# Normalising a column copy of x on GpSimd, with mean and rstd spread by DMA, in place of ScalarE's row form and TensorE's transposes

## The chip, the cores and the metric

One core of one Trainium2 chip. The metric is the device time of the whole kernel in microseconds, median over runs. Engines are named TensorE (PE in the rows, PEld its weight loads), VectorE (DVE), ScalarE (ACT), GpSimd (POOL) and SyncE (SP, which here only issues DMAs).

## The reference, cut to what matters

A block with cross attention and a top-2 mixture of experts. The change touches only how `_layernorm(x)` reaches the q projection of the attention.

```python
def _layernorm(x, axis=-1, eps=1e-05):
    m = jnp.mean(x, axis=axis, keepdims=True)
    v = jnp.var(x, axis=axis, keepdims=True)
    return (x - m) / jnp.sqrt(v + eps)

def _L0_xattn_ref(q, k, v, w_qs, w_ks, w_vs, w_proj, b_proj):
    qh = jnp.einsum('bld,hdk->hblk', q, w_qs)      # 16 heads, D = 256, d_k = 64
    kh = jnp.einsum('bld,hdk->hblk', k, w_ks)      # k, v: 64 rows of context per batch
    vh = jnp.einsum('bld,hdk->hblk', v, w_vs)
    attn = jax.nn.softmax(jnp.einsum('hblk,hbmk->hblm', qh, kh), axis=-1)
    out = jnp.einsum('hblm,hbmk->hblk', attn, vh) * qh
    out = out.transpose(1, 2, 0, 3).reshape(q.shape[0], q.shape[1], -1)
    return out @ w_proj.T + b_proj

x = x + jnp.tanh(g_xattn[0]) * _L0_xattn_ref(_layernorm(x), ctx_1024, ctx_1024, ...)
x = x + jnp.tanh(g_ffn[0]) * _L0_ffn_ref(_layernorm(x), ...)   # 8 experts, 2 per token
```

x is (4, 1024, 256) in float32.

## The kernel before, in words

The program has two stages. The first is the attention; the second runs 71 blocks of 128 routed rows through the experts. All of the change lies in the first.

**Tiling.** The 4096 tokens are cut into 8 groups `g` of 512 (`NG`), and each group into `TG` = 4 tiles of 128. The 16 heads make 8 pairs `p` (`NP`). One step of the attention handles pair `p` of group `g`, and every engine's program has a `step` function that is written out for all 64 steps. `n` is the running number of the pair. The steps are a hand-made software pipeline: in the step of pair n TensorE projects q for n, makes scores for n-1, transposes probabilities for n-4, multiplies by v for n-5 and projects out for n-6. Small jobs are hung on fixed steps of a group: layernorm of the next group, the second layernorm and routing of the group two back, and a piece of an expert's weights, split into two float16 halves, in each step.

**How the normalised x reaches q.** Rows of x are loaded to `xin`. VectorE takes statistics in `ln1` (four `bn_stats`, in step p = 1 for the next group) and `ln1_moments` (p = 2); GpSimd raises the variance to -1/2 in `ln_rstd` (p = 3); VectorE makes `shift` in `ln1_shift_of` (p = 4); ScalarE writes `xn` in `ln1_apply` (p = 4 and 5); TensorE transposes `xn` into the PSUM bank `job_ps` in `x_transpose` (ends of p = 5 and 6); ScalarE and VectorE take the high and low float16 halves `xt_h`, `xt_l` in `split_x` (p = 6 and 7), and `project_q` of the next group waits for the last `xt_lo`. In group 0 `job_ps` is also the bank of `project_k`, so that `project_k(6)` and `(7)` wait for `split_x` to have read it.

**VectorE's step**, in order: `residual` (p = 6), `exp_sum` for pair n-3 (`esum`, `rinv`), the small jobs, `score_max` and `score_sub` for pair n-1 (`smax`, `ssub`), `times_q` for n-5 (`r`), `expert_lo` (`split`). The small jobs of steps 3 and 4 are the two halves of `choose` (the routing, chains of ops on 128x32), that of step 5 is `place`. TensorE's `scores` for pair n-1 wait for `score_sub` of pair n-2, since `s_ps` is one buffer.

**GpSimd's step**: `normalize` for n-3 (`pn`), then `ln_rstd`, one `scatter` of records by an indirect DMA (from group 2 on), `product_lo` for n-5 (`r_l`), which waits for ScalarE's `r_h`. TensorE uses `pn` and `r_l` one step later.

**SyncE** issues in the order written in `group`; a wait in it holds all that follows.

Of the kernel before, what the change touches and what calls it, by code (L numbers as in the profile page):

```python
# [22 lines left out]
F32 = mybir.dt.float32  # L23
# [48 lines left out]
def build(nc, x, ctxt, g_xattn, g_ffn, wq, wk, wv, wproj, bproj, gate, w1, w2, out):  # L72
    dram = dict(
        x=x, ctxt=ctxt, g_xattn=g_xattn, g_ffn=g_ffn, wq=wq, wk=wk, wv=wv, wproj=wproj, bproj=bproj, gate=gate, w1=w1, w2=w2,
# [4 lines left out]
        w_split=nc.dram_tensor("w_split", (E, P, 2, WN), F16, kind="Internal").ap(),  # L79
    )  # L80
# [168 lines left out]
def attention(nc, ctx, dram, carry, weights):  # L249
# [41 lines left out]
    xn = sb("xn", [P, TG, D], F32)  # L291
# [26 lines left out]
    wp_sb = q32[:, 4:8, :].rearrange("p a g -> p (a g)").rearrange("p (c n) -> p c n", c=KD)  # L318

# [31 lines left out]
    ln1_ops, ln1_rstd, ln1_shift, xn_done, xt_tp, xt_hi, xt_lo = (sem(n) for n in ("ln1_ops", "ln1_rstd", "ln1_shift", "xn_done", "xt_tp", "xt_hi", "xt_lo"))  # L351
# [74 lines left out]
    def _(sp):  # L426
# [82 lines left out]
        for c in range(B // 2):  # L509
            double_v(c)  # L510
# [15 lines left out]
    def _(pe):  # L526
# [37 lines left out]
        def project_k(p):  # L564
# [114 lines left out]
        def small_job(g, k, p):  # L679

            if p == 1 and known(g, 2):
                x2_transpose(g - 2, k, 0)
# [67 lines left out]
    def _(act):  # L750
# [3 lines left out]
        def ln1_apply(g, par, tiles=range(TG)):  # L754
            if tiles[0] == 0:
                act.wait_ge(ln1_shift, g)
                after(act, xt_tp, 2 * g)
            for t in tiles:
                last = nc.scalar.activation(xn[:, t, :], xin[:, par, t, :], ACT.Identity, bias=shift[:, 0, t:t + 1], scale=rstd[:, 0, t:t + 1])
            if tiles[-1] == TG - 1:  # L760
                last.then_inc(xn_done, 1)

        def split_x(g, par, k, bank):

            act.wait_ge(xt_tp, 2 * g + k + 1)
# [17 lines left out]
        for k in range(KD):  # L783
            split_x(0, 0, k, (q_ps, pt_ps)[k])
# [86 lines left out]
        def step(b, g, k, p, pairs_back=LAST):  # L871
# [4 lines left out]
            if p in (6, 7) and has_next(g):  # L876
                split_x(g + 1, 1 - k, p - 6, job_ps)
# [54 lines left out]
    def _(dve):  # L932
# [22 lines left out]
        def ln1_shift_of(g):  # L955
            dve.wait_ge(ln1_rstd, g + 1)
            nc.vector.scalar_tensor_tensor(shift[:, 0, :], mv[:, 0, :, 0], -1.0, rstd[:, 0, :], ALU.mult, ALU.mult).then_inc(ln1_shift, 1)

        def split_x(g, par, k, bank):
# [20 lines left out]
        for k in range(KD):  # L980
            split_x(0, 0, k, (q_ps, pt_ps)[k])
# [111 lines left out]
        def step(b, g, k, p, pairs_back=LAST):  # L1093
# [82 lines left out]
    def _(pool):  # L1176
# [45 lines left out]

        def scatter(g, par, i):
# [10 lines left out]
        def step(g, k, p, pairs_back=LAST):  # L1234
# [474 lines left out]
```

## Time and profile before

| | |
|---|---|
| median of 3 runs | 795.76 us (794.93 to 798.36) |
| the profiled execution | 796.72 us, of which its span, first to last instruction, is 794.6 us |
| attention stage | about the first 370 us of the span |
| TensorE, VectorE, GpSimd, ScalarE busy over the span | 93%, 77%, 53%, 48% |
| mean granted TensorE clock | 0.987 of full speed |

Shares are averages over both stages. What a step costs is to be read inside the attention stage, in the stretches of single groups (a group lasts some 42 us), by who waits for whom.

### The profile page before, as it was taken

How to read it: one execution, taken by the hardware profiler on the slowest of the kernel's cores; microseconds unless marked ns; L12 is line 12 of the kernel's file. 1: busy time of each engine (PE TensorE's matmuls, PEld its weight loads, DVE VectorE, ACT ScalarE, POOL GpSimd, SP SyncE). 2: the span in 40 equal slices, each digit the busy share in tenths (PEclk: the TensorE clock that was granted, in tenths of full speed). 3: DMA queues.
4: the chain of work that ended last, by engine and by line, in shares of the span. 5: the costliest groups of instructions: out<-in, count | busy, mean ns of one | idle time of the engine just before them, and what ended most of it. 6: DMA issues, size and time to landing. Idle time of an engine off the chain costs nothing. (4 is left out here: it accounts for less than half of the span.)

```text
span 794.6 us, 23823 instructions
## 1 busy us (share of the span) xinstructions
PE 740.1 (93%) x8020; PEld 615.9 (78%) x8021; DVE 610.5 (77%) x1305; ACT 382.5 (48%) x680; POOL 417.3 (53%) x380
## 2 busy tenths in 40 slices
PE   4979999999999999987799998999999999999991
PEld 2657777676767777755798887899999999999991
DVE  6668889999898989794777778877777777777760
ACT  3566776767666676653344432333333333333330
POOL 3124454757676666645434475645555555555542
PEclk9999999999999999999899999999999999999997
DMA  8543242627272534423688866433333333333321
GB/s 268 160 108 132 80 161 92 234 81 265 74 255 93 208 113 175 139 100 87 207 217 229 233 161 125 76 54 47 48 52 50 49 46 53 50 50 47 51 32 20
DMA packets 94104, 93.74 MB, mean 118 GB/s; under 512 B 59216, under 2 KB 77840, under 8 KB 94032
## 3 DMA queue, kind: packets, MB, share of 16 engines
q1 hardware_dynamic: 32400, 65.89, 25.0%
q0 software_dynamic: 13392, 18.03, 13.0%
q10 hardware_dynamic: 48240, 8.87, 7.0%
q8 instruction: 43, 0.70, 0.4%
q14 instruction: 29, 0.24, 0.1%
HBM read 53.76 MB, written 37.95 MB: 115 GB/s over the span
## 5 line engine op out<-in xcount | busy, mean ns | idle before, releaser
L1399 PE MATMUL h_ps<-bx_h,w_now 128*128 128x128 f16 x2272 | 195.4, 220 | 12.5 <-DVE bx_l L1536 12.4
L1412 PE MATMUL pair_ps<-weights,ht_h 128*128 x1136 | 190.7, 273 | 2.5 <-DVE ht_l L1550 1.8
L1399 PEld LDWEIGHTS h_ps<-bx_h,w_now 128*128 128x128 f16 x2272 | 153.0, 98 | 17.3 <-DVE bx_l L1536 15.2
L1399 PE MATMUL h_ps<-bx_l,w_now 128*128 128x128 f16 x1136 | 157.0, 220 | 0.0
L1412 PE MATMUL pair_ps<-weights,ht_l 128*128 x568 | 154.9, 273 | 0.0
L1656 POOL DMA_INDIRECT out<-y,meta x71 | 144.3, 2032 | 15.7 <-issue 8.8
L1221 POOL TENSOR_TENSOR r_l<-r,r_h 128x512 f16<-128x512 f32 x64 | 74.3, 1161 | 104.8 <-ACT r_h L835 104.8
L1655 POOL TENSOR_TENSOR wait_mark<-wait_mark 128x1 f32<-128x1 f32 x71 | 40.3, 567 | 163.3 <-DMA out<-y,meta 101.9
L1412 PEld LDWEIGHTS pair_ps<-weights,ht_h 128*128 128x128 f16 x1136 | 110.0, 97 | 18.2 <-issue 3.6
L1475 ACT ACTIVATE y<-pair_ps,meta 128x256 f32<-128x256 f32 x71 | 33.6, 473 | 175.6 <-DVE bx L1525 75.8
L1548 DVE CAST ht_h<-hid 128x1024 f16<-128x1024 f32 x71 | 49.4, 696 | 73.2 <-ACT hid L1468 73.2
L1468 ACT ACTIVATE hid<-h_ps 128x1024 f32<-128x1024 f32 x71 | 72.5, 1022 | 51.1 <-PE h_ps L1399 51.1
L1550 DVE TENSOR_TENSOR ht_l<-hid,ht_h 128x1024 f16<-128x1024 f32 x71 | 87.0, 1226 | 2.4
L1399 PEld LDWEIGHTS h_ps<-bx_l,w_now 128*128 128x128 f16 x1136 | 87.6, 98 | 0.0
L1542 DVE COPY w_now<-weights 128x4096 f16 x71 | 86.8, 1222 | 0.0
L1215 POOL TENSOR_TENSOR pn<-ex,rinv 128x512 f32<-128x512 f32 x64 | 66.4, 1038 | 38.6 <-DVE rinv L1021 38.6
L609 PEld LDWEIGHTS s_ps<-kb,q 128*128 128x128 f32 x512 | 67.3, 193 | 13.8 <-issue 5.8
L609 PE MATMUL s_ps<-kb,q 128*128 128x128 f32 x512 | 68.6, 278 | 2.8 <-DVE ssub L1012 2.8
L651 PE MATMUL pair_ps<-wp_h,r_h 128*128 128x256 f16 x256 | 61.3, 275 | 2.5 <-DVE x_even L1034 2.4
L835 ACT CAST r_h<-r 128x512 f16<-128x512 f32 x64 | 39.4, 616 | 45.0 <-DVE r L1027 44.1
L651 PE MATMUL pair_ps<-wp_l,r_h 128*128 128x256 f16 x256 | 60.7, 273 | 0.0
L1412 PEld LDWEIGHTS pair_ps<-weights,ht_l 128*128 128x128 f16 x568 | 55.5, 98 | 5.2
(260 smaller groups left out, 1326.8 us busy)
## 6 DMA issues: line engine op xcount, KB each, us to landing
stage<-in_w SPq DMA_DIRECT2D x16, 1024.0 KB, 8.7
w_split<-split SPq DMA_DIRECT2D x14, 1024.0 KB, 6.1
weights<-w_split SPq DMA_DIRECT2D x14, 1024.0 KB, 5.9
rows<-records ACTq DMA_DIRECT2D x268, 32.0 KB
xin<-in_x SPq DMA_DIRECT2D x8, 512.0 KB, 4.9
x_even<-in_x SPq DMA_DIRECT2D x4, 512.0 KB, 3.6
x_odd<-in_x SPq DMA_DIRECT2D x4, 512.0 KB, 3.6
out<-x_even SPq DMA_DIRECT2D x4, 512.0 KB, 2.7
```

Of the source, the lines that this page charges most:

```text
L609: last = nc.tensor.matmul(s_ps[:, t].rearrange("p h m -> p (h m)"), q32[:, p, t * P:(t + 1) * P], kb[:, b, p, :] if isinstance(b, int) els ...
L651: nc.tensor.matmul(pj_ps[:, t, :], r_h[:, p % 2, t * P:(t + 1) * P], wt[:, p, :], start=(p == 0 and i == 0 and t % 2 == 0), stop=False, sk ...
L1215: nc.gpsimd.tensor_tensor(pn[:, p % 2].rearrange("p h t m -> p t h m"), ex[:, p % 2].rearrange("p t (h m) -> p t h m", h=2), rinv[:, p % 2 ...
L1221: nc.gpsimd.tensor_tensor(r_l[:, p % 2, :], r32[:, p % 2, :], r_h[:, p % 2, :], ALU.subtract).then_inc(r_lo, 1)
L1399: last = nc.tensor.matmul(h_ps[r % 2][:, c, :], w1_now[:, r % 2, s, k * F + c * P:k * F + c * P + P], xt[:, r % 2, k, :], start=(j == 0 an ...
L1412: last = nc.tensor.matmul(y_ps[r % 2], ht[:, r % 2, c, :], weights_at(e, s, WN // 2 + c * D, D).rearrange("p o n -> p (o n)"), start=(c == ...
L1468: nc.scalar.activation(hid[:, r % 2], h_ps[r % 2][:, :, :], ACT.Silu, scale=1.0 / WS).then_inc(h_act, 1)
L1542: nc.vector.tensor_copy(w1_now[:, r % 2], weights[:, bass.ds(e, 1), :, 0:KD * F].rearrange("p o s n -> p (o s) n")).then_inc(w1_ready, 1)
L1548: nc.vector.tensor_copy(ht_h[:, r % 2], hid[:, r % 2]).then_inc(h_hi, 1)
L1550: nc.vector.tensor_tensor(ht_l[:, r % 2], hid[:, r % 2], ht_h[:, r % 2], ALU.subtract).then_inc(h_lo, 1)
L1655: nc.gpsimd.tensor_tensor(wait_mark[:, 1:2], wait_mark[:, 0:1], wait_mark[:, 0:1], ALU.add).then_inc(mark_set, 1)
L1656: pool.indirect_dma_start(out, bass.IndirectOffsetOnAxis(meta[:, r, 0:1].bitcast(U32), 0), y[:, r % 2, :], None, compute_op=ALU.add).then_ ...
```

## The change

The host also gives x by columns: `xt[g, d, k, t, q]` in DRAM, so that one group is a tile `xt_in` of 128 partitions x (2 x 512). For groups 1 to 7:

- SyncE loads `xt_in` (`load_xt`, 512 KB), writes mean and rstd of the group (8 numbers per partition) to DRAM and, when that has landed, reads them back spread over all partitions as `mean_rstd` (128 x 1024 numbers, 512 KB; `spread_moments`).
- GpSimd subtracts the mean and multiplies by rstd in place: `centre_x` and `scale_x`, each a `tensor_tensor` on 128x512 once per half `k`, so four per group, in steps 3, 4, 5 and 6 (in group 0: two each in steps 5 and 6). The operand from `mean_rstd` is read with a step of 8 numbers.
- `split_x` on ScalarE and VectorE reads `xt_in` in SBUF in place of `job_ps` in PSUM.
- ScalarE's `ln1_apply`, VectorE's `ln1_shift_of` and TensorE's 14 calls of `x_transpose` go, with the waits around `job_ps`; group 0 still goes through `xn`.
- `ln1` moves from step 1 to step 0, `ln1_moments` from 2 to 1, `ln_rstd` from 3 to 1 (in group 0 they stay). SyncE's order within a group changes.

```diff
+        def load_xt(g):
+            if g == 1:
+                sp.wait_ge(xt_tp, KD)
+            else:
+                sp.wait_ge(xt_lo, KD * g)
+            sp.dma_start(xt_in[:, :, :], dram["xt"][g]).then_inc(xt_loaded, 16)
+
+        def spread_moments(g):
+            sp.wait_ge(ln1_rstd, g + 1)
+            row = dram["moments"][g % 2]
+            sp.dma_start(row.rearrange("(p n) -> p n", p=P), mv[:, 0, :, :].rearrange("p t s -> p (t s)")).then_inc(moments_out, 16)
+            sp.wait_ge(moments_out, 16 * g)
+            after(sp, x_normed, 2 * KD * (g - 1))
+            sp.dma_start(mean_rstd[:, :, :, :].rearrange("p q t s -> p (q t s)"), row.partition_broadcast(P)).then_inc(moments_in, 16)
...
         def group(g, par):
-            load_residual(g, par)
+            if known(g, 1) and has_next(g):
+                load_xt(g + 1)
             if not isinstance(g, int) or g + 2 < NG:
                 load_x(g + 2, par)
+            if known(g, 1) and has_next(g):
+                spread_moments(g + 1)
+            load_residual(g, par)
+            if known(g, HELD):
+                store_split(g, 0)
+            if has_next(g):
+                load_w1(g + 1)
             if known(g, 1):
                 store_x1(g - 1, 1 - par)
...
# TensorE
             after(pe, k_placed, 2 * p)
-            if p == 6:
-                pe.wait_ge(xt_lo, KD + 1)
-            if p == 7:
-                pe.wait_ge(xt_lo, 2 * KD)
...
-            if p == 5 and has_next(g):
-                x_transpose(g + 1, 0, job_ps)
-            if p == 6 and has_next(g):
-                x_transpose(g + 1, 1, job_ps)
...
# ScalarE
-            if p == 4 and has_next(g):
-                ln1_apply(g + 1, 1 - k, range(TG if first else TG // 2))
-            if p == 5 and has_next(g) and not first:
-                ln1_apply(g + 1, 1 - k, range(TG // 2, TG))
             if p in (6, 7) and has_next(g):
-                split_x(g + 1, 1 - k, p - 6, job_ps)
+                split_x(g + 1, 1 - k, p - 6, xt_in[:, p - 6, :])
...
# VectorE
-            if p == 4 and has_next(g):
-                ln1_shift_of(g + 1)
-            if p == 1 and has_next(g):
+            if p == (1 if first else 0) and has_next(g):
                 ln1_of(b, g, k)
-            if p == 2 and has_next(g):
+            if p == (2 if first else 1) and has_next(g):
                 ln1_moments(g + 1)
...
# GpSimd
+        def centre_x(g, k):
+            if k == 0:
+                pool.wait_ge(xt_loaded, 16 * g)
+                pool.wait_ge(moments_in, 16 * g)
+            x = xt_in[:, k, :].rearrange("p (t q) -> p t q", t=TG)
+            nc.gpsimd.tensor_tensor(x, x, mean_rstd[:, :, :, 0].rearrange("p q t -> p t q"), ALU.subtract).then_inc(x_normed, 1)
...
-            if p == 3 and has_next(g):
+            if p == (3 if g == 0 else 1) and has_next(g):
                 ln_rstd(0, g + 1, ln1_ops, ln1_rstd)
+            if p == (5 if g == 0 else 3) and has_next(g):
+                centre_x(g + 1, 0)
+            if p == (5 if g == 0 else 4) and has_next(g):
+                scale_x(g + 1, 0)
+            if p == (6 if g == 0 else 5) and has_next(g):
+                centre_x(g + 1, 1)
+            if p == 6 and has_next(g):
+                scale_x(g + 1, 1)
```

**GpSimd, steps 3, 4 and 5 of group 3, before.** `pn` opens each step and `r_l` ends it; the DMAs are the scatters.

```order
L1215 TENSOR_TENSOR pn<-ex,rinv 128x4x2x64
L1194 TENSOR_TENSOR rstd<-vare,minus_half 128x4
L1231 DMA records<-rec_odd,slot_odd 33920x258
L1221 TENSOR_TENSOR r_l<-r,r_h 128x512
L1215 TENSOR_TENSOR pn<-ex,rinv 128x4x2x64
L1231 DMA records<-rec_odd,slot_odd 33920x258
L1221 TENSOR_TENSOR r_l<-r,r_h 128x512
L1215 TENSOR_TENSOR pn<-ex,rinv 128x4x2x64
L1229 TENSOR_TENSOR wait_mark<-wait_mark 128x1
```

The same steps after the change:

```order
L1219 TENSOR_TENSOR pn<-ex,rinv 128x4x2x64
L1233 TENSOR_TENSOR xt_in<-xt_in,mean_rstd 128x512
L1249 DMA records<-rec_odd,slot_odd 33920x258
L1225 TENSOR_TENSOR r_l<-r,r_h 128x512
L1219 TENSOR_TENSOR pn<-ex,rinv 128x4x2x64
L1239 TENSOR_TENSOR xt_in<-xt_in,mean_rstd 128x512
L1249 DMA records<-rec_odd,slot_odd 33920x258
L1225 TENSOR_TENSOR r_l<-r,r_h 128x512
L1219 TENSOR_TENSOR pn<-ex,rinv 128x4x2x64
L1233 TENSOR_TENSOR xt_in<-xt_in,mean_rstd 128x512
L1247 TENSOR_TENSOR wait_mark<-wait_mark 128x1
```

One 128x512 operation (L1233 centres, L1239 scales) now stands right behind each `pn`; the small `rstd` op has gone to step 1.

**VectorE, step 4 of group 3, before**: the end of `exp_sum`, the shift, and the second half of `choose`.

```order
L1018 TENSOR_REDUCE esum<-ex 128x8
L1021 RECIPROCAL rinv<-esum 128x8
L957 SCALAR_TENSOR_TENSOR shift<-mv,rstd 128x4
L207 TENSOR_REDUCE top<-lg 128x4
L208 TENSOR_TENSOR cand<-lg,top 128x32
L209 SCALAR_TENSOR_TENSOR cand<-cand,iota_e 128x32
L210 TENSOR_REDUCE choice<-cand 128x4
L211 TENSOR_TENSOR mask<-iota_e,choice 128x32
```

The same place after:

```order
L1023 TENSOR_REDUCE esum<-ex 128x8
L1026 RECIPROCAL rinv<-esum 128x8
L209 TENSOR_REDUCE top<-lg 128x4
L210 TENSOR_TENSOR cand<-lg,top 128x32
L211 SCALAR_TENSOR_TENSOR cand<-cand,iota_e 128x32
L212 TENSOR_REDUCE choice<-cand 128x4
L213 TENSOR_TENSOR mask<-iota_e,choice 128x32
```

Only `shift` has gone; the chain of small routing ops is as it was.

**SyncE, from the second weight load of one group to the first store of the next, before:**

```order
L448 DMA stage<-in_w 128x8x256
L456 DMA x_odd<-in_x 128x1024
L460 DMA xin<-in_x 128x1024
L464 DMA out<-x_even 128x1024
L471 DMA w_split<-split 256x1x2048
```

and after:

```order
L455 DMA stage<-in_w 128x8x256
L471 DMA xt_in<-in_xt 128x1024
L486 DMA xin<-in_x 128x1024
L477 DMA moments<-mv 128x8
L480 DMA mean_rstd<-moments 128x1024
L463 DMA x_even<-in_x 128x1024
L497 DMA w_split<-split 256x1x2048
```

Two loads of x now follow the weight load at once, then the two transfers of the moments, and only then the residual and the next group's stores.

## Rows read from the trace of the kernel before

**Rows 1.** 125 to 165 us: busy PE, PEld, DVE, ACT, POOL, clock, DMA.

```profile
125.00:165.00 40.00, 39.64 (x342) 29.18 (x341) 36.69 (x99) 27.97 (x53) 25.53 (x26) 1.00 0.49 168
```

**Rows 2.** What TensorE waited for, 85 to 345 us: total, times, longest.

```profile
PE s_ps L609 <- DVE ssub L1012: 1.0, 5, 0.2
```

**Rows 3.** Timeline of TensorE, group 3: start, length, idle before.

```profile
175.66 0.71 PE L533 MATMUL job_ps<-ident,xn 128*128 128x128 f32 x4
176.21 0.59 PE L599 MATMUL q_ps<-xt_h,wq_h 128*128 128x512 f16 x2
...
180.84 0.65 PE L533 MATMUL job_ps<-ident,xn 128*128 128x128 f32 x4
181.32 0.60 PE L599 MATMUL q_ps<-xt_h,wq_h 128*128 128x512 f16 x2
...
187.61 1.13 PE L609 MATMUL s_ps<-kb,q 128*128 128x128 f32 x8 [0.20 <-DVE ssub L1012]
```

**Rows 4.** Timeline of VectorE, groups 2 (end) and 3.

```profile
151.02 1.35 DVE L942 BATCH_NORM_STATS2 stats<-xin 128x6 f32<-128x256 f32 x4
...
163.44 0.69 DVE L1007 TENSOR_REDUCE smax<-s_ps 128x8 f32<-128x512 f32 x1 [0.59 <-PE s_ps L609]
...
166.91 0.44 DVE L957 SCALAR_TENSOR_TENSOR shift<-mv,rstd 128x4 f32<-128x4 f32 x1
...
167.49 0.90 DVE L208 TENSOR_TENSOR cand<-lg,top 128x32 f32<-128x32 f32 x1
...
168.86 0.19 DVE L211 TENSOR_TENSOR mask<-iota_e,choice 128x32 f32<-128x32 f32 x1
...
173.23 1.09 DVE L232 TENSOR_TENSOR mask<-pos,mask 128x32 f32<-128x32 f32 x2
...
174.34 0.13 DVE L235 TENSOR_TENSOR seen<-seen,mtiles 128x8 f32<-128x8 f32 x1
...
183.57 0.64 DVE L962 TENSOR_TENSOR xt_l<-job_ps,xt_h 128x512 f16<-128x512 f32 x1
...
186.78 0.69 DVE L1012 TENSOR_TENSOR ssub<-s_ps,smax 128x512 f32<-128x512 f32 x1
```

**Rows 5.** Timeline of GpSimd, group 3.

```profile
160.86 1.04 POOL L1215 TENSOR_TENSOR pn<-ex,rinv 128x512 f32<-128x512 f32 x1
...
166.19 1.15 POOL L1221 TENSOR_TENSOR r_l<-r,r_h 128x512 f16<-128x512 f32 x1 [2.04 <-ACT r_h L835]
167.30 1.04 POOL L1215 TENSOR_TENSOR pn<-ex,rinv 128x512 f32<-128x512 f32 x1
...
173.14 1.03 POOL L1215 TENSOR_TENSOR pn<-ex,rinv 128x512 f32<-128x512 f32 x1
...
182.97 1.15 POOL L1221 TENSOR_TENSOR r_l<-r,r_h 128x512 f16<-128x512 f32 x1 [0.95 <-ACT r_h L835]
```

**Rows 6.** L208 in both stages: shortest, median, longest in ns, first and last start.

```profile
L208 DVE TENSOR_TENSOR cand<-lg,top x12: 191/340/902, 119.3 to 336.5; 128x32 f32<-128x32 f32 x12
L208 DVE TENSOR_TENSOR last_cand<-last_lg,last_top x4: 191/192/193, 416.4 to 460.0; 128x32 f32<-128x32 f32 x4
```

**Rows 7.** DMA issues, 140 to 170 us: size, us to landing.

```profile
stage<-in_w SPq DMA_DIRECT2D x1, 1024.0 KB, 8.7
x_odd<-in_x SPq DMA_DIRECT2D x1, 512.0 KB, 3.5
xin<-in_x SPq DMA_DIRECT2D x1, 512.0 KB, 4.5
```

**Rows 8.** SyncE's timeline: the weight load that ends group 2's issues.

```profile
147.02 0.61 SPq L448 DMA_DIRECT2D stage<-in_w  x1
```

**Rows 9.** Timeline of TensorE in group 0.

```profile
50.15 2.04 PE L574 MATMUL job_ps<-x2t,rec_even 128*128 128x256 f32 x4 [2.90 <-DVE xt_l L962]
...
59.12 1.10 PE L574 MATMUL job_ps<-x2t,rec_even 128*128 128x256 f32 x4 [1.35 <-DVE xt_l L962]
```

**Rows 10.** Timeline of VectorE at the start of group 1.

```profile
65.63 0.69 DVE L1018 TENSOR_REDUCE esum<-ex 128x8 f32<-128x512 f32 x1
```

More of the change, by code:

```diff
@@ L79, in build @@
         w_split=nc.dram_tensor("w_split", (E, P, 2, WN), F16, kind="Internal").ap(),
+        moments=nc.dram_tensor("moments", (2, G * 2), F32, kind="Internal").ap(),
     )
@@ L290, in attention @@
     shift = sb("shift", [P, 2, TG], F32)
-    xn = sb("xn", [P, TG, D], F32)
+    xt_in = sb("xt_in", [P, KD, G], F32)
+    mean_rstd = sb("mean_rstd", [P, P, TG, 2], F32)
     xt_h, xt_l = (sb(f"xt_{s}", [P, 2, KD, G], F16) for s in "hl")
@@ L318, in attention @@
     wp_sb = q32[:, 4:8, :].rearrange("p a g -> p (a g)").rearrange("p (c n) -> p c n", c=KD)
+    xn = xt_in[:, :, :].rearrange("p k g -> p (k g)").rearrange("p (t d) -> p t d", t=TG)
     ctx_t = x2t[:, :, 0:B // 2 * 3 * M].rearrange("p k (c j m) -> p k c j m", c=B // 2, j=3)
@@ L508, in _ @@
         load_w2(0)
-        for c in range(B // 2):
-            double_v(c)
+        load_xt(1)
+        double_v(0)
+        spread_moments(1)
+        double_v(1)
         for k in range(GB):
@@ L681, in small_job @@
             if p == 1 and known(g, 2):
+                if g > 2:
+                    pe.wait_ge(routed.pos_read, g - 2)
                 x2_transpose(g - 2, k, 0)
@@ L752, in _, with split_x @@
         nc.scalar.activation(esum[:, 0, 0, 0:1], ident[:, 0:1], ACT.Exp)
[L754 to L765, printed above, removed]
+        def split_x(g, par, k, x):
+            if g == 0:
+                act.wait_ge(xt_tp, k + 1)
+            else:
+                act.wait_ge(x_normed, 2 * (KD * (g - 1) + k + 1))
             if known(g, 2):
                 act.wait_ge(q_mm, pair_no(g - 2, NP))
-            nc.scalar.copy(xt_h[:, par, k, :], bank[:, :]).then_inc(xt_hi, 1)
+            nc.scalar.copy(xt_h[:, par, k, :], x).then_inc(xt_hi, 1)
         def split_wq(half):
@@ L783, in _ @@
         for k in range(KD):
[L784 removed]
+            split_x(0, 0, k, (q_ps, pt_ps)[k][:, :])
         split_wq(1)
@@ L946, in ln1_moments @@
             dve.wait_ge(ln1_ops, 3 * g + 1)
-            after(dve, xn_done, g)
+            after(dve, moments_out, 16 * (g - 1))
             nc.vector.memset(vare[:, 0, :], EPS)
@@ L953, in ln1_moments, with split_x @@
             nc.vector.tensor_tensor(vare[:, 0, :], vare[:, 0, :], mv[:, 0, :, 1], ALU.add).then_inc(ln1_ops, 1)
[L955 to L959, printed above, removed]
+        def split_x(g, par, k, x):
             dve.wait_ge(xt_hi, 2 * g + k + 1)
-            nc.vector.tensor_tensor(xt_l[:, par, k, :], bank[:, :], xt_h[:, par, k, :], ALU.subtract).then_inc(xt_lo, 1)
+            nc.vector.tensor_tensor(xt_l[:, par, k, :], x, xt_h[:, par, k, :], ALU.subtract).then_inc(xt_lo, 1)
         def split_wq(half):
@@ L1193, in ln_rstd @@
             pool.wait_ge(ops, 3 * g + 3)
-            nc.gpsimd.tensor_tensor(rstd[:, i, :], vare[:, i, :], minus_half[:, :], ALU.pow).then_inc(done, 1)
+            to = mv[:, 0, :, 1] if i == 0 and g > 0 else rstd[:, i, :]
+            nc.gpsimd.tensor_tensor(to, vare[:, i, :], minus_half[:, :], ALU.pow).then_inc(done, 1)
         def count_up(dst, pattern, channel):
```

33 lines of the change are left out of this document (15 added, 18 removed).

## The prediction

> **What bounds the kernel now.** I read the busy time by stretches first. In a stretch of 40 us of the attention TensorE is busy 39.6 us and VectorE 36.7 [rows 1]. By that alone TensorE bounds the attention, and whatever leaves it is gain. The second view says something finer: over 260 us TensorE waits five times, about once a group, 0.2 us each, always at `scores` for VectorE's `ssub` [rows 2]. So within a group there is a place where VectorE is as late as TensorE can bear.
>
> The timeline shows where. In step 3 of group 3 VectorE waits 0.59 us for TensorE's scores, at 163.44 [rows 4]: there VectorE is early. From then on it has no such wait until `ssub` of pair 7, which ends at 187.47 (186.78 + 0.69) [rows 4], and TensorE, 0.20 us late already, starts the scores at 187.61 [rows 3]. Steps 4 to 7 carry the routing, the residual, `xt_l` and the second layernorm's statistics, and VectorE needs 24.0 us for this stretch (163.44 to 187.47), just over what TensorE needs. The kernel is bound by TensorE in steps 0 to 3 and by VectorE in steps 3 to 7.
>
> The third thing to see is how long small operations take on VectorE. `cand` is 128x32. In the expert stage its four runs take 191 to 193 ns; in the attention the median is 340 and the longest 902 [rows 6]. At 167.49 it takes 0.90 us and ends at 168.39, just after GpSimd's `pn`, which ran from 167.30 to 168.34 [rows 4, 5]. `shift` before it ends at 167.35, as GpSimd's `r_l` does (166.19 + 1.15 = 167.34). The pair of `mask` products at 173.23 takes 1.09 us and ends at 174.32, after the `pn` that ends at 174.17. So a VectorE operation that reads two tiles in SBUF doesn't overlap a GpSimd operation that reads SBUF: it waits for its end, and a queue of both alternates, one by one.
>
> The Trainium skill, SBUF — State Buffer, Who interferes with whom, says this as a rule: a VectorE instruction with two SBUF inputs contends with a GpSimd one that reads SBUF, and "the second one to issue fully blocks until the first finishes". The rows above agree. By that rule the change is paid on VectorE, though VectorE's own list gets shorter.
>
> **What leaves TensorE.** 14 calls of `x_transpose`. The two of group 3 hold TensorE from 175.66 to 176.21 and from 180.84 to 181.32 [rows 3], 1.03 us a group. They lie inside VectorE's stretch, though, so TensorE would only arrive earlier at the wait of 187.61. Their worth in groups 2 to 6 is what VectorE's stretch gets shorter, and no more.
>
> **What leaves VectorE.** `shift`, 0.44 us, of which most was waiting for `r_l`. ScalarE loses `ln1_apply`; it bounds nothing in this stretch, so 0.
>
> **What comes to GpSimd.** Four operations a group on 128x512 float32 with two SBUF inputs. No row has their strided operand. The nearest is `pn`, 1.04 us, and `r_l`, 1.15 [rows 5]. I take d = 1.1 us. Bounds: 1.04 below, and 1.5 times `pn`, 1.56, as what a strided read might cost; that factor is my choice, about the middle between no penalty and twice as long. GpSimd is busy 25.5 of 40 us [rows 1]; with 4 x 1.1, about 30, it has room. The Trainium skill, GPSIMD Engine Reference, Performance pitfalls for Q7 kernels, gives about 2.9 cycles an element in place of 1.9 where the step is over 8 bytes; here it is 32, and that would be 1.56 us. No row shows it.
>
> **What this does to VectorE, group 3, one by one.**
> - Step 4. Without `shift`, `cand` waits for the end of `r_l`, the next op (L209) for the end of `pn` (168.34), and the comparison `mask` of L211 for the end of `scale_x`, which follows `pn` at once: 168.34 + 1.1 = 169.44 in place of 168.86 [rows 4, 5]: +0.58.
> - Step 5. `seen` starts at 174.34, 0.17 after `pn` ends. Now `centre_x` stands behind `pn`, and it waits for d: +0.93.
> - Step 6. `scale_x` runs while VectorE works on PSUM (`smax`, `ssub`, `r`): +0.05; 0.5 if d is 1.56.
> - Step 7. `xt_l` read a PSUM bank; it now reads two SBUF tiles. `r_l` ran from 182.97 to 184.12, beside `xt_l` at 183.57, without harm [rows 4, 5]. Behind `scale_x` and a scatter it is later by some 1.8 us, VectorE by some 1.5, so they meet again: +0.85, the rest of `r_l`.
>
> Sum 2.4 us a group, with 1.56 for d 3.8 (1.04 + 1.39 + 0.5 + 0.85). The lower bound is that nothing is held up and `shift`'s 0.44 is won. There are five such groups, 2 to 6: +12.0 us (-2.2 to +19).
> - `ln1`'s 1.35 us [rows 4] moves into step 0, behind the late stretch. TensorE then has a step of about 4.7 us against VectorE's 4.8, so 0.1 a group is lost, 0.5 in all.
>
> **Group 0.** Here TensorE waits 2.90 and 1.35 us in `project_k(6)` and `(7)` for `xt_l` to free `job_ps` [rows 9], and the first product after it takes 2.04 us against 1.10 for the second. With the two transposes up to 6.5 us could go. What is late next is VectorE, with three `expert_lo` pieces a step that read two SBUF tiles, beside four new GpSimd operations in two steps: `esum` of group 1, now at 65.63 [rows 10], comes by my walk along its ops between 61.3 and 62.7, and `ln1` costs 1.35 before the next scores. I take -3.7 (-6.5 to -1).
>
> **Group 1** has no routing: -0.5 (-1 to 0), since half of the transposes' 1.03 should be kept.
>
> **The transfers.** `xt_in` and the next `xin` follow the weight load issued at 147.02 (landing 8.7 later, 155.7 [rows 7, 8]). Two loads of 512 KB issued together landed within 4.5 us, so 3 to 4 us more: 159. The small write lands behind them at about 160, and the broadcast, priced as `x_odd`, 3.5 later: 163.7. GpSimd reaches `centre_x` at about 162, when `pn` of 160.86 is done [rows 5], and idles 2 us. That costs nothing: `r_l` of this step waited 2.04 us for ScalarE anyway, until 166.19 [rows 5], and the scatter still fits between. Without that cover each us more would delay `r_l` and then the output projection.
>
> **Sum.** 796.7 (profiled) + 12.0 + 0.5 - 3.7 - 0.5 = 805.0. The median of before lies 1.0 under the profiled time, so 804.
>
> **The rivals.**
> 1. The gain arrives. For it: TensorE's 99% and group 0's waits. Against: rows 2. If GpSimd's new operations fall between VectorE's two-input ones, the groups gain 0.44 each (2.2), group 1 1.0, group 0 up to 6.5: down to 786, likely 789. Chance 0.18. It decides at one point: if holding up costs under 0.9 us a group, the sum is a gain.
> 2. It cancels: one hold-up of about 0.9 to 1 us a group, not two or three, and group 0's 4. 796. Chance 0.14.
> 3. The strided read makes d 1.56: 5 x 3.8 in place of 12, group 0 at -1: 814. This is where the skill's figure above would lead. Chance 0.25.
> 4. The moments come 3 us later than I think, since the small write waits behind 3 MB; GpSimd then stalls in step 3, `r_l` is late and TensorE waits in steps 4 and 5, 1 to 2 us a group on top: 812. For it: the order of SyncE's queue. Against: 2 us of idle there now. Chance 0.05.
>
> My forecast, port hold-ups at d near 1.1, has 0.38; with rivals 3 and 4 "slower" holds 0.68. A change of 0.5%, about what can be told from none, is 4 us: faster 0.18, same 0.14, slower 0.68. Range: 789 to 817, which leaves out the best case of group 0 and what lies above rival 3; the forecast's own range is 799 to 810.
>
> **What would show it.** In the new profile: the new GpSimd ops at about 1.1 us; `mask` of L211's old place and `seen` with a duration near 1 us; TensorE's wait for `ssub` 3 us or more a group (2.4 + 1.03) in place of 0.2, with TensorE's busy share down; group 0's waits of 2.90 and 1.35 gone; no wait of TensorE for `r_l`. If TensorE still waits 0.2 us a group the forecast is wrong and rival 1 holds; if it waits for `pn` or `r_l`, GpSimd itself is the bound. Wrong most likely through VectorE: if two of its ops slip in where I let them alternate, half of the 12 us goes.

## The result: 822.7 us, slower by 3.3%

| | before | changed |
|---|---|---|
| median, us | 795.35 (794.57 to 798.36, 4 runs) | 822.74 (819.86 to 824.78, 4 runs) |
| ratio | | 1.0334 (95%: 1.0286 to 1.0383) |
| TensorE busy in the profiled execution, us | 740.1 | 740.4 |
| VectorE, GpSimd busy, us | 610.5, 417.3 | 646.1, 471.7 |

The forecast was 804 us, with a range of 789 to 817. The sign was right; the loss against the median of before is 27.4 us where I had 8, and the time lies outside the range.

Where it is lost shows in the windows of the changed kernel. They are cut at the issues of `x1`'s store, which come in step 6 of each group from 1 on: the first window is the end of group 0 and most of group 1, the others run from step 6 to step 6. Columns: the stretch, its length, then busy time of PE, PEld, DVE, ACT and POOL, granted clock, DMA share, GB/s.

```profile
46.05:92.04 45.99, 42.08 (x320) 29.05 (x319) 42.71 (x72) 27.49 (x53) 31.95 (x25) 0.96 0.48 163
92.04:137.86 45.82, 43.21 (x366) 30.80 (x364) 42.95 (x102) 28.01 (x52) 27.31 (x24) 1.00 0.45 153
137.86:185.94 48.08, 41.89 (x346) 29.33 (x346) 45.15 (x102) 26.97 (x51) 34.47 (x32) 1.00 0.48 165
185.94:233.22 47.28, 41.75 (x346) 29.35 (x346) 43.78 (x102) 26.96 (x51) 34.42 (x32) 1.00 0.49 168
```

The same cuts in the kernel before:

```profile
46.05:93.94 47.89, 43.64 (x335) 31.54 (x334) 37.38 (x72) 30.50 (x59) 19.84 (x18) 0.96 0.25 88
93.94:136.67 42.73, 42.55 (x364) 31.56 (x362) 38.90 (x103) 29.56 (x55) 20.44 (x20) 1.00 0.41 140
136.67:178.94 42.27, 41.91 (x358) 30.76 (x357) 38.91 (x103) 29.18 (x54) 27.56 (x28) 1.00 0.48 163
```

The first window wins 1.9 us, the next one (step 7 of group 1, then steps 0 to 5 of group 2) loses 3.1, and each one from then on 5.0 to 6.5; VectorE is busy for 4.9 to 6.4 us more there than in the last stretch of before, with about the same number of instructions. The granted clock is the same in both kernels in these stretches. In the waits of TensorE in the first 420 us (total, times, longest), the 0.2 us a group of [rows 2] have become

```profile
PE s_ps L637 <- DVE ssub L1017: 20.9, 15, 1.8
PE q_ps L627 <- DVE xt_l L967: 7.5, 7, 1.4
...
PE pair_ps L685 <- POOL r_l L1225: 3.1, 6, 0.9
PE job_ps L188 <- DVE mboth L219: 3.1, 4, 1.4
```

Now group 3 as in [rows 4, 5]. VectorE, the operations that got longer:

```profile
166.41 1.52 DVE L213 TENSOR_TENSOR mask<-iota_e,choice 128x32 f32<-128x32 f32 x1
...
172.19 0.97 DVE L211 SCALAR_TENSOR_TENSOR cand<-cand,iota_e 128x32 f32<-128x32 f32 x1
...
173.41 1.22 DVE L213 TENSOR_TENSOR mask<-iota_e,choice 128x32 f32<-128x32 f32 x1
...
178.84 2.47 DVE L234 TENSOR_TENSOR mask<-pos,mask 128x32 f32<-128x32 f32 x2
...
189.13 1.09 DVE L1065 SCALAR_TENSOR_TENSOR split<-stage,split 128x512 f16<-128x512 f32 x1
...
190.97 2.87 DVE L967 TENSOR_TENSOR xt_l<-xt_in,xt_h 128x512 f16<-128x512 f32 x1
```

and GpSimd beside them:

```profile
166.35 1.53 POOL L1233 TENSOR_TENSOR xt_in<-xt_in,mean_rstd 128x512 f32<-128x512 f32 x1 [0.48 <-DMA mean_rstd<-moments]
...
172.07 1.04 POOL L1219 TENSOR_TENSOR pn<-ex,rinv 128x512 f32<-128x512 f32 x1
173.07 1.51 POOL L1239 TENSOR_TENSOR xt_in<-xt_in,mean_rstd 128x512 f32<-128x512 f32 x1
...
178.75 1.04 POOL L1219 TENSOR_TENSOR pn<-ex,rinv 128x512 f32<-128x512 f32 x1
179.75 1.51 POOL L1233 TENSOR_TENSOR xt_in<-xt_in,mean_rstd 128x512 f32<-128x512 f32 x1
...
188.16 1.52 POOL L1239 TENSOR_TENSOR xt_in<-xt_in,mean_rstd 128x512 f32<-128x512 f32 x1
...
191.12 1.17 POOL L1225 TENSOR_TENSOR r_l<-r,r_h 128x512 f16<-128x512 f32 x1
192.24 1.05 POOL L1219 TENSOR_TENSOR pn<-ex,rinv 128x512 f32<-128x512 f32 x1
```

Set the ends beside each other. The first `mask` ends at 167.93, `centre_x` (L1233) at 167.88. `cand` ends at 173.16, `pn` at 173.11; the second `mask` at 174.63, `scale_x` (L1239) at 174.58; the pair of products at 181.31, the second `centre_x` at 181.26. Each time VectorE comes free 0.05 us after GpSimd. `xt_l` ends at 193.84, which is 0.55 after the end of `pn` at 193.29: it waited through `r_l` and through `pn`, and then did its own work. It does so once in each of groups 2 to 6.

The longest hold-up in the attention is of a small operation, in step 4 of group 5: `cand` on 128x32 waits through three GpSimd operations.

```profile
266.39 3.67 DVE L210 TENSOR_TENSOR cand<-lg,top 128x32 f32<-128x32 f32 x1
```

```profile
266.37 1.17 POOL L1225 TENSOR_TENSOR r_l<-r,r_h 128x512 f16<-128x512 f32 x1
267.49 1.04 POOL L1219 TENSOR_TENSOR pn<-ex,rinv 128x512 f32<-128x512 f32 x1
268.49 1.51 POOL L1239 TENSOR_TENSOR xt_in<-xt_in,mean_rstd 128x512 f32<-128x512 f32 x1
```

### The profile page after: what moved, and what is told of

Read it like the earlier page. It is cut to its first block and busy times, and to the rows that moved or that the text cites. A ratio compares the mean times of both kernels' runs of the same rounds, so it can differ in the third digit from the quotient of the medians.

```text
span 822.9 us, 23721 instructions
## 1 busy us (share of the span) xinstructions
PE 740.4 (90%) x7964; PEld 608.5 (74%) x7965; DVE 646.1 (79%) x1298; ACT 368.1 (45%) x652; POOL 471.7 (57%) x408
## 3 DMA queue, kind: packets, MB, share of 16 engines
q1 hardware_dynamic: 35424, 73.26, 26.8%
q0 software_dynamic: 13392, 18.03, 12.6%
## 5 line engine op out<-in xcount | busy, mean ns | idle before, releaser
L1682 POOL DMA_INDIRECT out<-y,meta x71 | 150.3, 2117 | 15.7 <-issue 9.0
L1681 POOL TENSOR_TENSOR wait_mark<-wait_mark 128x1 f32<-128x1 f32 x71 | 35.7, 502 | 160.5 <-DMA out<-y,meta 102.6
L1225 POOL TENSOR_TENSOR r_l<-r,r_h 128x512 f16<-128x512 f32 x64 | 76.1, 1188 | 66.1 <-ACT r_h L848 65.8
L1501 ACT ACTIVATE y<-pair_ps,meta 128x256 f32<-128x256 f32 x71 | 33.6, 474 | 173.9 <-DVE meta L1557 62.7
L1219 POOL TENSOR_TENSOR pn<-ex,rinv 128x512 f32<-128x512 f32 x64 | 69.7, 1089 | 42.3 <-DVE rinv L1026 42.3
L637 PEld LDWEIGHTS s_ps<-kb,q 128*128 128x128 f32 x512 | 65.5, 192 | 36.8 <-issue 31.8
L679 PE MATMUL pair_ps<-wp_h,r_h 128*128 128x256 f16 x256 | 61.3, 275 | 3.7 <-DVE x_even L1039 2.9
```

The costliest lines, as they stand in the source:

```text
L637: last = nc.tensor.matmul(s_ps[:, t].rearrange("p h m -> p (h m)"), q32[:, p, t * P:(t + 1) * P], kb[:, b, p, :] if isinstance(b, int) els ...
L679: nc.tensor.matmul(pj_ps[:, t, :], r_h[:, p % 2, t * P:(t + 1) * P], wt[:, p, :], start=(p == 0 and i == 0 and t % 2 == 0), stop=False, sk ...
L1219: nc.gpsimd.tensor_tensor(pn[:, p % 2].rearrange("p h t m -> p t h m"), ex[:, p % 2].rearrange("p t (h m) -> p t h m", h=2), rinv[:, p % 2 ...
L1225: nc.gpsimd.tensor_tensor(r_l[:, p % 2, :], r32[:, p % 2, :], r_h[:, p % 2, :], ALU.subtract).then_inc(r_lo, 1)
L1682: pool.indirect_dma_start(out, bass.IndirectOffsetOnAxis(meta[:, r, 0:1].bitcast(U32), 0), y[:, r % 2, :], None, compute_op=ALU.add).then_ ...
```

## The experiments

Theory A: all of the loss is VectorE waiting behind GpSimd in operations with two SBUF inputs. Its rivals: B, the round trip of the moments through DRAM; C, the larger loads by columns and the earlier place of `ln1`; A2, any further GpSimd operation costs VectorE its length, wherever it stands; D, GpSimd's own program is too long. The ratio is to the kernel before on the same chip.

| run | built on | median us | ratio (95%) |
|---|---|---|---|
| small_ops | changed | 791.97 | 0.9929 (0.9902 to 0.9957) |
| packed | changed | 815.67 | 1.0221 (1.0189 to 1.0253) |
| behind_scatter | changed | 834.17 | 1.0468 (1.0417 to 1.0518) |
| low_from_psum | changed | 810.16 | 1.0163 (1.0120 to 1.0206) |
| moments_once | changed | 823.00 | 1.0316 (1.0269 to 1.0364) |
| timed | changed | 818.71 | 1.0255 (1.0220 to 1.0289) |
| timed_ahead | changed | 805.50 | 1.0104 (1.0076 to 1.0132) |
| timed_psum | changed | 794.95 | 0.9975 (0.9944 to 1.0006) |
| timed_late_low | changed | 797.72 | 1.0020 (1.0000 to 1.0040) |
| extra_ops | before | 809.79 | 1.0151 (1.0119 to 1.0183) |
| extra_ops_low | before | 825.39 | 1.0356 (1.0308 to 1.0404) |
| low_only | before | 799.97 | 1.0026 (0.9997 to 1.0055) |
| early_pair | before | 791.51 | 0.9917 (0.9885 to 0.9949) |
| early_pair_5 | before | 792.42 | 0.9935 (0.9912 to 0.9957) |

**Take the work out, leave the rest.**

```diff
-            x = xt_in[:, k, :].rearrange("p (t q) -> p t q", t=TG)
+            x = xt_in[:, k, :].rearrange("p (t q) -> p t q", t=TG)[:, :, 0:1]
```

> The changed kernel with the four new subtractions and multiplications of each group made 4 columns wide instead of 512 (the column tiles of groups 1 to 7 are normalised in 4 columns only; all waits, transfers and the order stay). Theory A (the new GpSimd operations keep VectorE from its tiles while they run): all of the per-group loss of 5.7 us goes, 5 x 5.7 = 28 us and some of group 1: 788 to 794 us. Rival B (the round trip of the moments through DRAM, with the wait ahead of the first subtraction, sets the pace): the waits stay as they are, so 815 to 823 us. Rival C (the larger loads by columns, 7 MB more, or the earlier place of the row moments on VectorE): also 815 to 823 us.

791.97 us: the loss is gone, with every transfer, wait and move still there. B and C are out as causes of anything large.

> The changed kernel with the moments spread by DMA only once, for group 1; groups 2 to 7 are normalised with group 1's mean and rstd. The new GpSimd operations stay, their wait for a transfer in step 3 and the per-group DMAs go. Rival B (the round trip through DRAM sets the pace): 5 groups x up to 2 us, 812 us. Theory A: the first subtraction starts up to 2 us earlier and meets other VectorE operations, the number of operations is the same: 818 to 825 us.

823.0 us (ratio 1.0316, 1.0269 to 1.0364): nothing won that can be told from none. The wait for `mean_rstd` is real (0.48 us above, 3.7 us in three waits between 85 and 370 us), but `r_l` behind it waits for ScalarE in any case: in group 3 it has 1.91 us of that left.

**Put the work into the kernel before.** In `extra_ops` one call is added to GpSimd's step, on a tile that is dead by then, with a zeroed tile of the shape of `mean_rstd` as second input:

```diff
+            if g > 0 and p in (3, 4, 5, 6) and has_next(g):
+                extra_op()
```

> The kernel before with one thing added: four GpSimd subtractions of 128 x 512 with the strided second input, in steps 3, 4, 5 and 6 of groups 1 to 6, on tiles that nothing else uses by then. No column input, no moments in DRAM, the TensorE transposes and their evictions stay. Theory A (these operations alone cost the time): 5 to 6 groups x 3.5 to 5 us, 812 to 825 us. Rivals B and C (moments, loads, move of the row moments): nothing of theirs is in it, so 795 to 799 us.

809.79 us: the added operations alone cost 12.8 us against the kernel before on that chip (796.98), just short of the range. They are the cause of about half. `xt_l` still reads PSUM there and keeps its 0.64 us; whether that is the other half is what the next run asks.

> The kernel before with the four extra GpSimd subtractions per group (as in the run extra_ops, which took 809.8 us) and with xt_l of groups 3 to 7 computed from an SBUF tile instead of from the PSUM tile (their low halves are meaningless). Theory A with its two parts (extra operations, and one more VectorE operation that they can hold): 809.8 + 5 x 2.2 = 821 us, the time of the changed kernel. If the source of xt_l does not matter: 810 us.

```diff
-            nc.vector.tensor_tensor(xt_l[:, par, k, :], bank[:, :], xt_h[:, par, k, :], ALU.subtract).then_inc(xt_lo, 1)
+            source = xn[:, 2 * k:2 * k + 2, :].rearrange("p t d -> p (t d)") if known(g, 2) else bank[:, :]
+            nc.vector.tensor_tensor(xt_l[:, par, k, :], source, xt_h[:, par, k, :], ALU.subtract).then_inc(xt_lo, 1)
```

825.39 us. The kernel before, with these two additions and nothing else of the change, is as slow as the changed kernel. (This edit, and the control below, give the SBUF tile to groups 2 to 7, not 3 to 7 as the expectations say: `known(g, 2)` stands inside a call whose g is already the next group.) The exchange of one input cost 15.6 us, not 11. Without the extra operations it must cost little:

> The kernel before with xt_l of groups 3 to 7 computed from an SBUF tile instead of from the PSUM tile (their low halves are meaningless), and no extra GpSimd operations: the control for the run with both, which took 825.4 us. In the changed kernel with 4 columns wide operations xt_l met r_l of GpSimd and took 1.10 instead of 0.64 us: 5 x 0.5 = 2.5 us, 797 to 800 us. Theory A needs it far below the 15.6 us that the exchange cost in the presence of the extra operations; if the SBUF source costs by itself, 812 us.

799.97, ratio 1.0026: 1.7 us above the kernel before on that chip, at the edge of what can be told from none. The two parts do not just add up: alone they cost 12.8 and 1.7 us, together 28.2 (797.19 to 825.39). The reverse, in the changed kernel:

> The changed kernel with one input of one VectorE operation exchanged: the subtraction that makes xt_l reads the PSUM tile job_ps instead of the SBUF tile xt_in, for groups 3 to 7 (the low halves of these groups then hold meaningless numbers). Theory A (a VectorE operation with two SBUF inputs is held while GpSimd works, one with a PSUM input is not): the 2.87 us of the second xt_l in the profile of the changed kernel fall to 0.64, 2.2 us per group for five groups, and up to 1 us more where the projection of q waited for it: 808 to 813 us. Rival D (the loss sits in the length of GpSimd's own program, which is 54 us busier): 820 to 824 us.

810.16: -12.6 us for one input of one operation. D is out, since GpSimd's work is the same. What `xt_l` took in the changed kernel and in this run (count, shortest/median/longest in ns, first and last start):

```profile
L967 DVE TENSOR_TENSOR xt_l<-xt_in,xt_h x14: 639/643/2873, 51.1 to 335.0; 128x512 f16<-128x512 f32 x14
```

```profile
L967 DVE TENSOR_TENSOR xt_l<-job_ps,xt_h x10: 637/640/641, 137.2 to 321.3; 128x512 f16<-128x512 f32 x10
L967 DVE TENSOR_TENSOR xt_l<-xt_in,xt_h x4: 639/641/817, 49.7 to 95.7; 128x512 f16<-128x512 f32 x4
```

**Make the new operations shorter.**

> The changed kernel with the second input of the new operations read contiguously instead of with its stride (the columns are normalised with wrong elements of the spread moments). Theory A: one operation falls from 1.52 to about 1.04 us, and VectorE is kept waiting that much less, at least 5 groups x 4 x 0.48 = 10 us and up to 15, since some hold-ups no longer meet: 808 to 813 us. Rival B or C: under 3 us less, 819 to 823 us.

```diff
-mean_rstd[:, :, :, 0].rearrange("p q t -> p t q")
+mean_rstd[:, :, :, :].rearrange("p q t s -> p (q t s)")[:, 0:G].rearrange("p (t q) -> p t q", t=TG)
```

815.67: -7.1 us, between the two ranges. The operation fell to 1.27 us only, not to 1.04:

```profile
L1233 POOL TENSOR_TENSOR xt_in<-xt_in,mean_rstd x14: 1257/1267/1280, 44.8 to 319.3; 128x512 f32<-128x512 f32 x14
```

With 5 x 4 x 0.25 = 5 us as the direct part, and more where hold-ups no longer meet, this fits theory A; my figure for the contiguous operation was too low.

**Move them, with nothing left out.** First behind the scatter:

> The changed kernel with the new operations issued behind the scatter of their GpSimd step, just before that step waits for r_h, instead of ahead of it; the result is the same. Theory A in the finer form (what counts is which VectorE operation is next when one of them starts): behind the scatter VectorE works on PSUM tiles for longer, so steps 3 and 4 lose less, 1.5 to 3 us per group: 808 to 816 us. Rival A2 (any 128 x 512 GpSimd operation costs VectorE its length wherever it stands): 820 to 825 us. Rival B (moments): the first subtraction has 1 us more for its moments, so up to 5 us less in all, 818 us.

834.17: wrong in sign, 11.4 us slower still. The reason in step 5 of group 3, VectorE and then GpSimd in this run:

```profile
184.81 2.82 DVE L1065 SCALAR_TENSOR_TENSOR split<-stage,split 128x512 f16<-128x512 f32 x1
```

```profile
184.43 1.54 POOL L1233 TENSOR_TENSOR xt_in<-xt_in,mean_rstd 128x512 f32<-128x512 f32 x1
185.91 1.17 POOL L1225 TENSOR_TENSOR r_l<-r,r_h 128x512 f16<-128x512 f32 x1
```

The weight split (two SBUF inputs, 0.68 us by itself) is now the operation that is caught, and as `xt_l` above it waits through two GpSimd operations in a row, 2.1 us. So place decides. The next run uses that: each new operation starts with `smax`, when three VectorE operations with a PSUM input follow.

```diff
+            if p in (3, 4, 5, 6) and known(g, 1) and has_next(g):
+                max_starts(g, n, p)
+                (centre_x, scale_x)[(p - 3) % 2](g + 1, (p - 3) // 2)
```

`max_starts` waits for `s_mm` (the scores of this step) and for the last routing or `xt_l` operation that VectorE does ahead of `smax`. Group 0 is as in the changed kernel.

> The changed kernel with the same new GpSimd operations, same length, same number, same result, but in groups 1 to 6 each of them stands behind the scatter of its step and starts only when VectorE starts its row maximum (smax): the three VectorE operations that follow (smax, ssub, r) each have a PSUM input, and the next with two SBUF inputs, the weight split, starts 1.92 us after smax. Theory A (only the meeting of a GpSimd operation with a VectorE operation of two SBUF inputs costs): 1.52 us fit into that stretch, so nearly all of the loss goes: 792 to 798 us, as with the four columns wide operations (792.0). Rival A2 (a 128 x 512 GpSimd operation costs VectorE its length wherever it stands): 820 us or more. If PSUM operations are held too, or if the start comes 0.4 us late: 800 to 810 us.

818.71: in none of the three ranges. In steps 3 and 4 it works. VectorE's step from `smax` to `smax`:

```profile
164.95 0.69 DVE L1012 TENSOR_REDUCE smax<-s_ps 128x8 f32<-128x512 f32 x1 [0.58 <-PE s_ps L637]
...
170.56 0.68 DVE L1012 TENSOR_REDUCE smax<-s_ps 128x8 f32<-128x512 f32 x1
...
176.40 0.68 DVE L1012 TENSOR_REDUCE smax<-s_ps 128x8 f32<-128x512 f32 x1
...
178.33 2.81 DVE L1065 SCALAR_TENSOR_TENSOR split<-stage,split 128x512 f16<-128x512 f32 x1
...
185.56 3.45 DVE L1065 SCALAR_TENSOR_TENSOR split<-stage,split 128x512 f16<-128x512 f32 x1
```

```profile
165.38 1.52 POOL L1233 TENSOR_TENSOR xt_in<-xt_in,mean_rstd 128x512 f32<-128x512 f32 x1 [0.81 <-DMA mean_rstd<-moments]
...
171.03 1.54 POOL L1239 TENSOR_TENSOR xt_in<-xt_in,mean_rstd 128x512 f32<-128x512 f32 x1
...
177.94 1.53 POOL L1233 TENSOR_TENSOR xt_in<-xt_in,mean_rstd 128x512 f32<-128x512 f32 x1
```

5.61 and 5.84 us a step, where the kernel before has 5.83 and 5.85, with an operation of 1.5 us in each: A2 is out. In step 5 the scatter ahead of it kept the operation until 177.94, 1.54 us after `smax`, and it caught the split again, with `r_l` behind it. In step 6 the split (185.56, 3.45 us) began while the scatter ran and waited through `scale_x` and `r_l` as well. So these two go ahead of the scatter:

```diff
+            if p in (5, 6) and known(g, 1) and has_next(g):
+                max_starts(g, n, p)
+                (centre_x, scale_x)[(p - 3) % 2](g + 1, (p - 3) // 2)
             if p >= 5 and known(g, 2):
                 scatter(g - 2, k, p - 5)
```

> As the run timed (818.7 us), in which the new operations of steps 3 and 4 cost nothing (the step takes 5.84 us from smax to smax, as in the kernel before) and those of steps 5 and 6 came 1.5 us after smax, because the scatter stood ahead of them, met the weight split and kept it 2.1 and 2.8 us with the r_l behind them. Here those two stand ahead of the scatter, right behind pn; steps 3 and 4 are unchanged. Theory A: the operation of step 5 starts with smax and is over before the split, that of step 6 starts 0.95 us after smax (behind pn) and keeps the split about 0.6 us: of 4.9 us per group some 1 is left, 6 groups x 1 us above the 792.0 of the 4 columns wide operations: 796 to 800 us. Rival A2 (an operation costs its length wherever it stands, steps 3 and 4 were luck): 815 us or more.

805.50: 13.2 us won, 5.5 us above the range expected. Step 5 is clean now and the split of step 6 takes 1.09 us as expected; but the scatter, `r_l` and `pn` behind the operation of step 6 are late and meet `xt_l`:

```profile
185.18 2.87 DVE L967 TENSOR_TENSOR xt_l<-xt_in,xt_h 128x512 f16<-128x512 f32 x1
```

```profile
185.33 1.17 POOL L1225 TENSOR_TENSOR r_l<-r,r_h 128x512 f16<-128x512 f32 x1
186.44 1.05 POOL L1219 TENSOR_TENSOR pn<-ex,rinv 128x512 f32<-128x512 f32 x1
```

Is this one operation all that is left?

> The run timed_ahead (805.5 us) with xt_l of groups 3 to 7 read from the PSUM tile job_ps (their low halves are meaningless). All four new GpSimd operations, the transfer of the moments and the larger loads stay. In timed_ahead only the last of the four still cost: the second xt_l took 2.87 us, since it waited through r_l and the pn behind it. Theory A: 5 x 2.2 us less, and something for its followers: 792 to 796 us, the time of the 4 columns wide operations (792.0). If something else of the change costs as well (moments, loads, the place of the row moments), or a VectorE operation can't be held by two GpSimd operations in a row: 800 to 805 us.

794.95, ratio 0.9975 (0.9944 to 1.0006): yes. All that the change added is in this kernel but the source of one operand in groups 3 to 7, and its time can't be told from that of before. The last run leaves nothing out and moves `xt_l` by one place:

> The run timed_ahead with the same result, and two calls exchanged in step 7 of VectorE for groups from 1 on: the second xt_l stands behind the second layer norm's moments (bn_stats with one input, 1.4 us) instead of ahead of them, so that these run while GpSimd does r_l and pn. Theory A: xt_l then waits 0.5 to 1 us instead of 2.2, at 6 groups x 1.4 us: 796 to 800 us. If the projection of q, which waits for xt_l, then is what is late: 803 to 806 us.

```diff
-            if p in (6, 7) and has_next(g):
+            if (p == 6 or first and p == 7) and has_next(g):
                 split_x(g + 1, 1 - k, p - 6, xt_in[:, p - 6, :])
@@
                 ln2(g - 1, 1 - k)
+                split_x(g + 1, 1 - k, 1, xt_in[:, 1, :])
```

797.72, in the range expected. In group 3 the second `xt_l` now keeps its own length, and the longest of groups 1 to 7 is 0.74 us:

```profile
184.42 0.68 DVE L967 TENSOR_TENSOR xt_l<-xt_in,xt_h 128x512 f16<-128x512 f32 x1
```

So the change costs 0.2% (0.0 to 0.4) instead of 3.3% when it is placed so. That is no gain, though.

**The gain by itself.** The only part of the change that won was group 0, and it doesn't need the column input:

```diff
+                if g == 0:
+                    pe.wait_ge(v_placed, B)
+                    for half in range(KD):
+                        x_transpose(1, half, spare_bank(half))
...
-            if p == 6:
-                pe.wait_ge(xt_lo, KD + 1)
-            if p == 7:
-                pe.wait_ge(xt_lo, 2 * KD)
```

`spare_bank` gives two banks of `pj_ps`, which the first output projection has not yet used.

> The kernel before with only group 0 rearranged (same result): both tiles of group 1 are transposed at the end of step 5 into two PSUM banks that are still unused, and both split in step 6, so that the k projections of steps 6 and 7 no longer wait for the eviction of a transpose. No column input. The two waits of 2.90 and 1.35 us in group 0 were the gain that the changed kernel was to have there: 791 to 793 us if they are on the path, 796 if the work that follows was late anyway.

> The same kernel as early_pair (791.5 us, ratio 0.9917 to the kernel before), timed again in more rounds beside timed_ahead: 790 to 793 us, a ratio of 0.990 to 0.995; if the first result was an accident of the chip, 795 us.

791.5 and 792.4, ratios 0.9917 and 0.9935, with nothing left out: this kernel is faster than the kernel before by 0.7 to 0.8%, a small gain, but both intervals lie below 1. The waits of 2.90 and 1.35 us of [rows 9] are gone, and the last weight load of the scores starts at 354.1 us in place of 359.6: 5.5 us in the profiled execution. The medians differ by 5.7 and 4.2 us.

## Why the prediction was right in sign and three times too small

- **What bounds the kernel** (TensorE in steps 0 to 3, VectorE in 3 to 7): held. What VectorE lost came out as TensorE's waits, for `ssub` above all.
- **The mechanism**: its first half held, that a VectorE operation with two SBUF inputs waits for a GpSimd one; extra_ops, extra_ops_low and timed_psum show it from both sides. Its second half, that the two engines then alternate "one by one", failed: see step 7.
- **d, 1.1 us**: too low. 1.52 measured (28 operations, 1.51 to 1.54 but for two in group 0 that VectorE held). My upper bound was 1.56. The estimate worked out from the Trainium skill, GPSIMD Engine Reference, Performance pitfalls for Q7 kernels, was the same, but that it came so near is partly luck: contiguous, the operation takes 1.27 (packed), not the 1.04 of `pn`, and the stride costs 20%, not the 50% of that page.
- **Step 4, +0.58**: from `smax` to `smax` 6.70 us (168.19 to 174.89) against 5.83 (163.44 to 169.27): +0.87. **Step 5, +0.93**: 7.22 against 5.85, +1.37. It was not `seen` but the second `mask` product that waited, for the same `centre_x`. The two misses, 0.29 and 0.44, are about the 0.42 by which d was too low. **Step 6, +0.05**: from `smax` to `smax` 5.10 in both, but `scale_x` of this step starts at 188.16, after that `smax`, and outlasts the PSUM operations: it holds the weight split of 189.13, 1.09 us in place of 0.68, +0.41. The 0.5 that I had for d = 1.56 was the right size.
- **Step 7, +0.85**: from `smax` to `smax` 8.48 us (187.21 to 195.69) against 5.84, +2.64. The split above has 0.41 of it and `xt_l` the other 2.23 (2.87 in place of 0.64). This is the term that failed most, 1.4 us of the 3.3 missing per group. It rests on my sentence that a queue of both "alternates, one by one", by which `xt_l` would have waited for the rest of `r_l` and gone ahead of `pn`. It waited through both; so did the weight split, through two operations, in behind_scatter and timed, and `xt_l` again in timed_ahead. The Trainium skill, SBUF — State Buffer, Who interferes with whom, says that the later one waits until the first finishes (the words that the prediction quotes stand in that page's section Summary: rules for kernel authors); the rows here show that this may not be the end of the wait.
- **Step 3, 0**: wrong. I let `centre_x` idle for its moments until 163.7 and looked only at what that did to GpSimd. It ran at 166.35, into `choose`: `mask` took 1.52 us in place of 0.19, +1.33, of which the 0.59 us in which VectorE was early [rows 4] swallowed a part; +0.75 was left.
- The sum by steps, 3 to 7, is 0.75 + 0.87 + 1.37 + 0.41 + 2.23 = 5.6 us a group in place of 2.4; four stretches of 48.08, 47.28, 48.78 and 47.98 us against 42.3 give 5.7, and the one that holds steps 3 to 5 of group 2, but step 7 of group 1, in which `xt_l` waits 0.2 us only, gives 3.1 (0.75 + 0.87 + 1.37 = 3.0).
- **`ln1`'s move, +0.1**: not tried alone. The 792.0 us of small_ops hold it together with what group 0 gains there, so no run gives its size.
- **Group 0, -3.7**: -1.1, by `esum` of group 1, which starts at 64.50 in place of 65.63 [rows 10]; I had it between 61.3 and 62.7. TensorE's two waits went, as forecast. But the three weight splits of a step took 4.24 and 4.18 us there, where the kernel before has 1.90 for the same three, beside the new GpSimd operations, and TensorE got new waits, 1.42 us for `xt_l` and 0.92 for `r_l`. early_pair shows what was to be had without that: 4 to 6 us.
- **Group 1, -0.5**: the other 0.8 us of the first window, by subtraction only, so within my range.
- The account up to the last scores: -1.9 + 3.1 + 23.0 (the four stretches) + 2.6 (the last step 7) = 26.8 us; their last weight load starts at 386.5 us in place of 359.6, 26.9 later. The two profiled spans differ by 28.3 us (822.9 and 794.6); the 1.4 us that fall behind the last scores are within what single executions of one kernel differ by.
- **Transfers**: the moments' write landed at 162.4 and the broadcast at 166.3, 2.6 us later than the 163.7 forecast (group 3, where the changed kernel is 1.2 us later by the cut at 137.86); moments_once shows no cost of it.
- **Rivals**: 1 (the gain arrives) is false for the change but true for small_ops, 3 was nearest (814) and still lacked the wait through two operations, 4 is out. The range ended at 817, because I took rival 3's four hold-ups as the worst; one in step 3 and one behind two GpSimd operations in a row had no place in it.

**What stays open.** When a VectorE operation gets in between two GpSimd operations. In small_ops `xt_l` came 0.61 us after `r_l` had started, took 1.10 us, and kept `pn` for 0.45 us (1.49 in place of 1.04):

```profile
177.81 1.10 DVE L967 TENSOR_TENSOR xt_l<-xt_in,xt_h 128x512 f16<-128x512 f32 x1
```

```profile
177.20 1.15 POOL L1225 TENSOR_TENSOR r_l<-r,r_h 128x512 f16<-128x512 f32 x1 [0.46 <-ACT r_h L848]
178.32 1.49 POOL L1219 TENSOR_TENSOR pn<-ex,rinv 128x512 f32<-128x512 f32 x1
```

With the same neighbours, but 0.15 us ahead of `r_l` and while a scatter was still running, it waited through both (2.87). The order of arrival alone does not decide: the split of behind_scatter came 0.38 us after `centre_x` had started and waited through `r_l` as well (2.82). Nor does the width: in the changed kernel the 128x32 `cand` of 172.19 got in at the seam of `pn` and `scale_x`, and the one of 266.39 waited through three operations (3.67). No run here varies one of these things by itself. And TensorE's busy time is the same 740 us in the page of both kernels though 14 calls of `x_transpose` left it; matmul ends are modelled, and nothing here rests on it.

## What to carry to other kernels

Before work goes to GpSimd, list what VectorE does in the same stretch, and mark each operation that reads two SBUF tiles: a further GpSimd operation costs nothing beside PSUM readers (timed, steps 3 and 4) and beside the others up to its own length, or more where the next GpSimd operations follow at once. An edit that turns a PSUM input into an SBUF one is no free swap: here one such input was worth 12.6 us beside the new GpSimd operations, and 1.7 us, hardly told from none, without them. If the work must go there, tie its start to the first of a run of PSUM readers, and check what stands behind it in GpSimd's queue, since that arrives later and catches the next one.

## What was not expected of the hardware

- A waiting VectorE operation with two SBUF inputs does not always get in between two GpSimd operations. On 128x512 it took 2.81, 2.82 and 2.87 us in place of 0.64 to 0.68, and 3.45 where a scatter stood ahead (step 6 in timed and behind_scatter). A 128x32 one took 3.67 in place of 0.19.
- It works both ways: in group 0 GpSimd's `scale_x` took up to 2.03 us in place of 1.52 and `r_l` 1.60 in place of 1.15, beside VectorE's weight splits.
- A GpSimd operation of 128x512 in float32 with two full inputs, written over one of them, takes 1.27 us when all is contiguous and 1.52 with a step of 32 bytes in one input; `pn`, whose second input is broadcast, takes 1.04.
